# Moving seven bf16 weight casts behind the input loads on the GpSimd DMA queue of an eight-core cumulative-mean and slot-routing kernel

## The reference

```python
x = x + _layernorm(causal_mean(_layernorm(x)))              # causal_mean = softmax(tril zeros) @ x
x = x + _layernorm(ffn(_layernorm(x)))

# ffn(x), S = slot_init for every batch, slot_mean = S.mean over the slots
h = gelu(concat([x, slot_mean]) @ w1 + b1)                   # w1 is 2048 x 512
alpha = softmax over the top 8 of (h @ w2 + b2) / (|tau| + 0.1), zero elsewhere
si = (alpha.T @ x) / alpha.sum(tokens)
gi = si @ Wih.T + bih;  gh = S @ Whh.T + bhh                 # GRU: S_new from gi, gh, S
y = layernorm(S_new + attention(S_new; wq, wk, wv))
out = (alpha @ (y @ wvp + bvp)) @ wo + bo
```

## Time and profile before

| | us |
|---|---|
| Runs, median of 2 | 1253.34 (1249.6 and 1257.09) |
| Profiled execution, its own time | 1249.3 |
| Its span (first to last instruction of the slowest core) | 1247.7 |
| Spans of the eight cores | 1226.2 to 1247.7 |
| Busy: PE, DVE, ACT, POOL | 419.9, 320.8, 226.4, 165.2 |
| HBM read, written | 68.72 MB, 36.70 MB |

### The profile page before, as it was taken

How to read it: one execution, slowest core, us unless ns; L and a number is a source line. 1 busy time by engine, 2 the same in 40 slices (tenths; PEclk the granted TensorE clock), 3 DMA queues, 4 the chain that set the end, 5 groups by cost and what they waited for, 6 DMA issues and landing times.

```text
span 1247.7 us, 8868 instructions; the slowest of 8 cores (1226.2 to 1247.7 us)
## 1 busy us (share of the span) xinstructions
PE 419.9 (34%) x2610; PEld 192.8 (15%) x2610; DVE 320.8 (26%) x1080; ACT 226.4 (18%) x298; POOL 165.2 (13%) x91
## 2 busy tenths in 40 slices
PE   0000000034444444402888877533322364111110
PEld 0000000000000000001666655311111111000000
DVE  0000000034443444485100011455601011323322
ACT  0000000023233333301222233111100001222221
POOL 2000000012233222400000000100000000433443
PEclk9999999985555555555855599655555555555555
DMA  8999999910000000010111112000153322113113
GB/s 215 167 119 121 122 122 120 202 67 0 0 1 1 1 0 0 0 25 1 27 26 26 26 39 39 1 1 0 25 108 81 92 66 68 68 67 131 71 68 134
DMA packets 69294, 76.40 MB, mean 61 GB/s; under 512 B 53216, under 2 KB 57312, under 8 KB 68640
## 3 DMA queue, kind: packets, MB, share of 16 engines
q0 software_dynamic: 4800, 22.25, 15.6%
q1 hardware_dynamic: 64448, 53.60, 15.3%
HBM read 68.72 MB, written 36.70 MB: 84 GB/s over the span
## 4 chain that ended last, share of the span: by engine, by line
PE 26%; DVE 25%; another core or an unknown queue 20%; ACT 10%; issue 8%; DMA 6%; POOL 3%; DVEq 1%; ACTq 1%; POOLq 0%; SPq 0%
DVE bn6x L192 10%; PE p_h L539 8%; DVE bn6c L192 3%; ACT fnb L207 3%; POOL sb_x L1113 3%; DMA whhT<-wih_bf 3%; PE pcs L384 3%; PE pcs L392 2%; PE p_h L543 2%; DVE x2bf L178 2%; ACT anb L207 1%; PE p_f L1072 1%; PE p_xt L529 1%; ACT x3b L207 1%
## 5 line engine op out<-in xcount | busy, mean ns | idle before, releaser
L410 POOL TENSOR_TENSOR sb_x<-anb,sb_x 128x1024 f32<-128x1024 f32 x32 | 75.7, 2384 | 443.7 <-ACT anb L207 443.7
L539 PE MATMUL p_h<-x3t,sb_w1a 128*128 128x128 bf16 x1024 | 107.2, 268 | 37.7 <-DVE x3t L195 23.4
L1113 POOL TENSOR_TENSOR sb_x<-fnb,sb_x 128x1024 f32<-128x1024 f32 x32 | 74.8, 2337 | 133.2 <-ACT fnb L207 133.2
L539 PEld LDWEIGHTS p_h<-x3t,sb_w1a 128*128 128x128 bf16 x1024 | 79.7, 120 | 52.8 <-issue 43.8
L362 PE MATMUL p_init<-s_tri,sb_Sbf 64*128 64x1 bf16 x8 | 0.3, 162 | 255.0 <-DMA sb_w1b<-w 255.0
L384 PE MATMUL pcs<-x1b,s_tri 128*128 128x512 bf16 x64 | 32.7, 615 | 143.4 <-ACT anb L207 139.1
L1072 PE MATMUL p_f<-sb_sv,sb_alphaT 64*128 64x512 bf16 x64 | 32.1, 606 | 144.9 <-ACT fnb L207 143.5
L192 DVE BATCH_NORM_STATS2 bn6x<-sb_x 128x6 f32<-128x512 f32 x128 | 77.5, 678 | 0.0
L192 DVE BATCH_NORM_STATS2 bn6c<-pcs 128x6 f32<-128x512 f32 x64 | 39.9, 685 | 134.6 <-PE pcs L392 129.3
L192 DVE BATCH_NORM_STATS2 bn6x<-p_f 128x6 f32<-128x512 f32 x64 | 39.9, 685 | 117.6 <-PE p_f L1072 117.6
L195 DVE COPY x3t<-p_xt 128x1024 bf16<-128x1024 bf16 x32 | 22.1, 691 | 181.0 <-PE p_xt L529 181.0
(11 more groups left out here) (173 smaller groups left out, 580.2 us busy)
## 6 DMA issues: line engine op xcount, KB each, us to landing
sb_x<-x SPq DMA_DIRECT2D x8, 2048.0 KB, 130.2
out<-sb_x SPq DMA_DIRECT2D x8, 2048.0 KB, 6.6
whh_bf<-Whh POOLq DMA_DIRECT2D x1, 6144.0 KB, 99.3
wih_bf<-Wih POOLq DMA_DIRECT2D x1, 6144.0 KB, 158.7
wv_bf<-wv POOLq DMA_DIRECT2D x1, 2048.0 KB, 187.2
wvp_bf<-wvp POOLq DMA_DIRECT2D x1, 2048.0 KB, 206.4
wo_bf<-wo POOLq DMA_DIRECT2D x1, 2048.0 KB, 223.9
wst<-wv_bf SPq DMA_DIRECT2D x8, 256.0 KB, 2.7
```

Of the source, the lines that this page charges most:

```text
L410: g.tensor_tensor(sb_x[:, j * D:(j + 1) * D], anb[:, (j % 2) * D:(j % 2 + 1) * D], sb_x[:, j * D:(j + 1) * D], op=OP.add).then_inc(sX2, 1)
L539: t.matmul(ph[:, jc * P:(jc + 1) * P], w1av[:, dc, jc * P:(jc + 1) * P], x3tv[:, dc * P:(dc + 1) * P], start=(jc == 0 and dc == 0), stop=F ...
L1113: g.tensor_tensor(sb_x[:, j * D:(j + 1) * D], fnb[:], sb_x[:, j * D:(j + 1) * D], op=OP.add).then_inc(sX5, 1)
```

## The change

The seven casts leave the first block of POOL and come after slot_init and sb_w1b in the second. Ahead of them POOL now waits for all eight chunks of x. No other instruction changes; the lines below the edit move by two.

```diff
             g.dma_start(out=sb_bz[:], in_=w_d["bhh"].rearrange("(o j) -> o j", o=1)).then_inc(semGz, 16)
-            if stage >= 2:
-                g.dma_start(out=whh_bf, in_=w_d["Whh"]).then_inc(semGh, 16)
-                g.dma_start(out=wih_bf, in_=w_d["Wih"]).then_inc(semGw, 16)
-                g.dma_start(out=wq_bf, in_=w_d["wq"]).then_inc(semGq, 16)
-                g.dma_start(out=wk_bf, in_=w_d["wk"]).then_inc(semGq, 16)
-                g.dma_start(out=wv_bf, in_=w_d["wv"]).then_inc(semGq, 16)
-                g.dma_start(out=wvp_bf, in_=w_d["wvp"]).then_inc(semGq, 16)
-                g.dma_start(out=wo_bf, in_=w_d["wo"]).then_inc(semGq, 16)
...
             g.dma_start(out=sb_w1b[:].rearrange("p (c j) -> p c j", j=DH),
                         in_=w_d["w1"][D:2 * D, :].rearrange("(c p) j -> p c j", p=P)).then_inc(semGi, 16)
+            if stage >= 2:
+                for ch in range(8):
+                    g.wait_ge(semX[ch], 16)
+                g.dma_start(out=whh_bf, in_=w_d["Whh"]).then_inc(semGh, 16)
+                g.dma_start(out=wih_bf, in_=w_d["Wih"]).then_inc(semGw, 16)
+                g.dma_start(out=wq_bf, in_=w_d["wq"]).then_inc(semGq, 16)
+                g.dma_start(out=wk_bf, in_=w_d["wk"]).then_inc(semGq, 16)
+                g.dma_start(out=wv_bf, in_=w_d["wv"]).then_inc(semGq, 16)
+                g.dma_start(out=wvp_bf, in_=w_d["wvp"]).then_inc(semGq, 16)
+                g.dma_start(out=wo_bf, in_=w_d["wo"]).then_inc(semGq, 16)
```

## The result

| | before | after |
|---|---|---|
| Median of all runs, us | 1256.24 (10 runs, 1248.34 to 1272.96) | 1066.25 (11 runs, 1054.13 to 1077.42) |
| Profiled execution, us | 1249.3 | 1063.88 |
| Its span, slowest core, us | 1247.7 (core 1) | 1062.3 (core 7) |

The ratio is 0.8453, with a 95% interval from 0.8403 to 0.8503. The ratio says 15.5% faster; the medians differ by 190 us, 15.1%. The forecast was 1059 with a range from 1040 to 1092. The sum made against the profiled execution said 1055.6; the profiled execution of the changed kernel took 1063.9.

What follows compares the result with a forecast made beforehand. The prediction took the sb_w1b load, queued behind seven casts, to bound the kernel: 1249.3 less 193.7 gives 1055.6, plus 4.0 from profiled execution to median gives 1059.6, forecast 1059, range 1040 to 1092.

Steps and rivals of the forecast that it cites:

- The bound: At the kernel's start everything waits for the 1 MB load sb_w1b, queued behind seven casts on POOL; first piece 254.75 us.
- Turns by row: With POOL's and SP's DMA queues full, one row of each goes in turn, whatever its weight; a cast row takes 5.0 us.
- The head: Start up to the first matmul: sb_w1b lands at 61.1, first matmul moves from 254.99 to 61.3, saving 193.7 us.
- the tiny rows: 32 tiny rows in POOL's queue between sb_w2 and sb_bz, given 1 us ahead of sb_w1b's landing.
- The bound with the whole gap kept: Upper case for sb_w1b's landing: queue goes on from sb_bz at 44.7 instead of sb_w2 at 38.5, giving 66.3 us.
- x: SP's eight-chunk input load: all in at about 75.5 to 76 us, with DVE waiting for no chunk.
- The new wait: POOL waits for x before its casts, free at about 79.6, before its first add is wanted at 83.8; cost 0.
- The casts beside compute, and the fetches: Casts run beside the cumulative stage until about 264, ahead of their readers; instruction fetches cost 0, up to 35 us; chance 0.12.
- Everything after, and the sum: Stages behind 255 us only shift, some 8 us either way for core spread; sum 1055.6 plus 4.0 gives 1059.6.
- The slow pace of sb_w1a: Rival at the start: sb_w1b loads at sb_w1a's 29.2 us, first matmul at 75.4, total 1073; chance 0.08.
- sb_w1b alone: Rival at the start: sb_w1b loads in 5.3 us as if alone, landing at 45.1, total 1043; chance 0.06.
- held by its casts: Rival on POOL: cast issues block it until the last cast lands at 264, first add 164 late, total 1223; chance 0.04.

Runs made afterwards that it cites:

- e2: Kernel before, casts still ahead of slot_init and sb_w1b, but POOL waits for all eight chunks of x before the casts; 1268.37 us, ratio 1.0066.
- e3: Kernel before, with each of the seven casts issued in short rows of 1024 (or 256) elements rather than 16384; 1267.4 us, ratio 1.0107.
- e1: Changed kernel without the eight waits for x, casts still behind sb_w1b; 1073.9 us, ratio 0.8539 against the kernel before.
- e7: Changed kernel with the two small vectors sb_b2row and sb_bz issued behind sb_w1b rather than ahead of slot_init; 1071.4 us in one run.
- e4: Changed kernel with slot_init and sb_w1b issued ahead of sb_w1a, sb_w2, sb_b2row and sb_bz; 1042.84 us, ratio 0.8316 against the kernel before.
- e8: Changed kernel with POOL held behind its casts until the last five of them have landed; 1234.6 us, ratio 0.9787 against the kernel before.
- e9: Changed kernel unaltered, run again on another chip; 1067.35 us, ratio 0.8487 against the kernel before.
- e10: Changed kernel without the eight waits for x, run on the same chip as the repeat of the changed kernel; 1074.73 us, ratio 0.8523.

## Why the prediction was right, point by point

**The bound.** Right. The head of the chain was a 1 MB load behind seven casts in a queue served in order. e2 and e3 kept that order and changed the waits or the rows, and the time stayed within 2% of before (the upper end for e3 is 1.7%); e1 changed the order alone and gained 186 us by the medians on its chip.

**Turns by row.** Right in kind, and shown by e3: with rows of one sixteenth x arrived 140 us earlier, and the count of packets rose by the count of rows. "One row of each goes in turn" was too exact: x got some more (chunk 5 in e1).

**The head, 61.3 expected, 64.1 measured.** The mechanism was right, a term was mis-sized. sb_w2's landing (38.5 by the sum, 37.4) and the pace of sb_w1b behind slot_init (20.3 by the sum, 20.4) held. The step that failed is "I take sb_w2's landing, 38.5, as the moment from which the queue goes on", with 1.3 for slot_init and 1 for the tiny rows: 2.3 us from sb_w2 to slot_init, and it was 6.0 (5.9 on the mean of the eight cores). The prediction laid the gap behind sb_w2 before to the heavy cast rows beside it; it is there without them. Nor do the tiny vectors explain it: with them out of the way (e7) slot_init and sb_w1b land when they did, and it is sb_w2's own landing that moves. So sb_w2's landing was no good mark for where the queue stood, and what fills those us stays open. The bound with the whole gap kept, 66.3, is near what the cores showed: sb_w1b landed at 62.6 to 67.7 on the 16 cores profiled with the changed kernel, 66.0 on the mean, and the 63.9 of the slowest core is among the early ones.

**x.** All in at 77.3, 76 expected, with some luck: at sb_w1b's landing x had some 2960 rows and not 2624, and the rest came more slowly than the 5.3 us a chunk of the sum would have it (13.4 us for 1136 rows).

**The new wait.** Free, as said. First add at 86.2 (83.8 plus the later head), POOL ready at 81.4. Its slack was tested from both sides: e4 shortened the head and paid 10.8 us, e8 lengthened the wait and paid 156.0 of 178.3.

**The casts beside compute, and the fetches.** From the first statistics to the routing stage it took 323.3 us before and 322.8 after, and 323.1 both times on the mean of the cores. The price of instruction fetches behind cast rows is 0 within a microsecond; the upper bound of 35 was not needed.

**Everything after, and the sum.** The sum missed the profiled execution by 8.3 us: 2.8 in the head, 6.4 in the routing stage, less some tenths elsewhere. The step that carries this is "so I allow some 8 us either way for another draw". It was the right term, and it covered this draw, but as a bound it was too small. Over the twelve profiles the routing stage took from 184.6 to 225.9 us on a core, and the slowest core's took from 211.6 (the kernel before) to 225.9; the stage behind it took 100.0 to 100.2 on every core whose rows I read. The profiled execution of before had the shortest of these draws, and more runs moved the median of before from 1253.34 to 1256.24. Carrying over 4.0 us from the two runs shown made up for just over half of this 6.9. There is luck in how near the rest comes: the ratio on the median of before gives a gain of 194 us, the very 193.7 of the sum, but its interval runs from 188 to 201, and the traces put the head at 190.9 on the slowest core and 188.9 on the mean.

**The rivals.** The slow pace of sb_w1a did not occur, since the head's pace was that of sb_w1b beside x. sb_w1b alone did not occur: x had rows waiting all the time, and e2 shows what the pace is without them, 6.7 us. POOL was not held by its casts: seven issues took 3.6 us in all.

## What to carry to other kernels

A queue served in order is a priority list: put what the first instruction waits for at its head, and bulk that is read hundreds of microseconds later behind it. When a wait is added on an engine with other work behind it, work out up to which time it is free; here it was free by 22 us, and a further improvement of the head (e4) paid 10.8 us for it. A gap between two landings is not yet the cost of what stands between them: compare the landings themselves, on all cores, before one transfer is blamed for it (e7). Where one stage's length is drawn anew on each core and each run, read a gain of ten microseconds from the trace up to that stage, on the mean of the cores, not from the device time.

## What the runs showed of the hardware that was not expected

- The same 1 MB load took 6.7 us behind slot_init with nothing in the other queue (e2) and 20.4 beside x (the changed kernel); before, a cast row took 5.0 us on its engine, and x got 32 rows on each engine between the landings of chunks 3 and 4 (105.0 and 228.6), in which 25 cast rows pass.
- When two transfers of 16 tiny rows each no longer stood behind sb_w2, its landing moved from 39.1 to 42.9 us on the mean of eight cores, while slot_init's stayed at 45 (e9 and e7). No run tells why.
- The routing stage of one program took 191.8 and 218.0 us on two cores in the same execution, at a mean granted clock of 0.83 and 0.66. Why one core is granted more than the other stays open; no experiment was made on it.
- In e10, without the waits, the landing of sb_w1b differed by 7.7 us between cores 0 and 1 (56.7 and 64.4 us from issue), where e1, the same kernel, had 60.1 and 61.5. The changed kernel had 56.6 and 60.9 in one profile and 61.7 and 59.8 in the other. How cores share the first 60 us varies from run to run, and no experiment tells why.
